# Half-row-block strips with rows of up to 6 KB, 256-column matmuls and row sums spread over three sweeps, in a Chebyshev and SAGE graph kernel

## The reference

```python
h = jnp.maximum(_layernorm(x, axis=-1), 0.0)
terms = [h, adj @ h]
for _ in range(2, 4):
    terms.append(2.0 * (adj @ terms[-1]) - terms[-2])
x = x + jnp.einsum('kni,kio->no', jnp.stack(terms), w_cheb)
h = jnp.maximum(_layernorm(x, axis=-1), 0.0)
deg = jnp.clip(jnp.sum(adj, axis=1, keepdims=True) + 1.0, 1.0, None)
h_neigh = (adj @ h + h) / deg
z = relu(jnp.concatenate([h, h_neigh], axis=1) @ w_sage + b_sage)
x = x + z / jnp.maximum(jnp.linalg.norm(z, axis=1, keepdims=True), 1e-12)
```

## Time and profile before

| | |
|---|---|
| Median of 3 runs | 2655.51 us (2654.42 to 2662.23) |
| Profiled execution | 2672.75 us, its span 2670.9 us |
| PE busy | 2152.7 us (81%) |
| DVE busy | 1637.1 us (61%) |
| ACT busy | 730.2 us (27%) |
| Data read | 686 MB, 258 GB/s over the span |

### The profile page before, as it was taken

One profiled execution on the slowest core, in us unless ns is written; L12 is line 12 of the kernel. 1 busy time (PEld: TensorE's weight loads), 2 busy tenths in 40 slices (PEclk: granted clock), 3 DMA queues, 4 the chain that ended last, 5 costly groups with the idle time before them and its releaser, 6 DMA issues.

```text
span 2670.9 us, 20670 instructions
## 1 busy us (share of the span) xinstructions
PE 2152.7 (81%) x6792; PEld 919.9 (34%) x6792; DVE 1637.1 (61%) x1204; ACT 730.2 (27%) x2243; POOL 821.6 (31%) x1521
## 2 busy tenths in 40 slices
PE   0567778888999999989988979889886897776666
PEld 0123233333334444444434434333332343222222
DVE  2755556656656565756564566766575655576766
ACT  1766666666676674000000000000000000000000
POOL 2222223222322323323222434233232332233423
PEclk9988989999999999999999999889998998888878
DMA  9999999999999999999999999999999999999994
GB/s 206 259 261 265 274 262 268 274 270 268 269 277 276 266 262 258 234 272 238 265 248 259 252 261 257 268 250 269 276 254 268 264 272 267 271 264 270 248 258 127
DMA packets 326445, 689.56 MB, mean 258 GB/s; under 512 B 56514, under 2 KB 93378, under 8 KB 326338
## 3 DMA queue, kind: packets, MB, share of 16 engines
q1 hardware_dynamic: 216832, 344.03, 56.8%
q0 software_dynamic: 108672, 344.03, 46.1%
q10 hardware_dynamic: 834, 0.20, 0.0%
HBM read 685.97 MB, written 2.10 MB: 258 GB/s over the span
## 4 chain that ended last, share of the span: by engine, by line
PE 30%; DMA 29%; SPq 28%; ACT 5%; DVE 5%; issue 2%; POOL 0%; DVEq 0%; ACTq 0%
DMA ring<-in_adj_dram 28%; SPq L317 27%; PE ps_pair L745 23%; ACT ring L393 5%; PE ps_single L751 4%; DVE ring L601 3%; SPq L306 1%; DMA res<-in_x_dram 1%; PE ps_lin L690 0%; PE ps_lin L693 0%; PE ps_lin L706 0%; PE ps_tr L709 0%; PE ps_lin L698 0%; PE ps_xt L642 0%; PE ps_single L652 0%
## 5 line engine op out<-in xcount | busy, mean ns | idle before, releaser
L601 DVE STREAM_TRANSPOSE ring<-ring 128x2048 f32<-128x2048 f32 x640 | 1431.6, 2284 | 810.2 <-DMA ring<-in_adj_dram 536.6
L745 PE MATMUL ps_pair<-ring,vec 128*128 128x512 f32 x2880 | 1319.3, 616 | 151.8 <-DVE ring L601 140.4
L351 POOL DMA_DIRECT2D ring<-in_adj_dram x1448 | 786.0, 551 | 1811.9 <-PE ps_pair L745 1131.1
L745 PEld LDWEIGHTS ps_pair<-ring,vec 128*128 128x128 f32 x2880 | 559.4, 198 | 878.6 <-issue 766.5
L751 PE MATMUL ps_single<-ring,vec 128*64 128x512 f32 x2240 | 591.1, 665 | 285.2 <-DVE ring L601 281.2
L393 ACT ACTIVATE ring<-ring 128x512 f32<-128x512 f32 x1024 | 628.0, 615 | 297.3 <-DMA ring<-in_adj_dram 297.3
L751 PEld LDWEIGHTS ps_single<-ring,vec 128*64 128x64 f32 x2240 | 159.6, 149 | 644.9 <-issue 423.9
L420 ACT ACTIVATE sum_s<-ps_single 128x512 f32<-128x512 f32 x64 | 37.7, 590 | 616.7 <-PE ps_pair L745 449.5
L393 ACT ACTIVATION_READ_ACCUMULATOR ring<-ring 128x1 f32 x1024 | 192.0, 188 | 0.0
L422 ACT ACTIVATE sum_p<-ps_pair 128x512 f32<-128x512 f32 x45 | 26.6, 591 | 452.2 <-PE ps_pair L745 452.2
L431 ACT ACTIVATE stat<-stat 128x4 f32<-128x4 f32 x16 | 3.3, 205 | 258.7 <-DVE stat L554 258.7
(11 more groups left out here) (95 smaller groups left out, 576.7 us busy)
## 6 DMA issues: line engine op xcount, KB each, us to landing
ring<-in_adj_dram POOLq DMA_DIRECT2D x1160, 256.0 KB, 12.1
ring<-in_adj_dram SPq DMA_DIRECT2D x1160, 256.0 KB, 18.4
ring<-in_adj_dram POOLq DMA_DIRECT2D x96, 192.0 KB, 11.2
ring<-in_adj_dram SPq DMA_DIRECT2D x96, 192.0 KB, 18.6
ring<-in_adj_dram POOLq DMA_DIRECT2D x96, 128.0 KB, 10.9
ring<-in_adj_dram SPq DMA_DIRECT2D x96, 128.0 KB, 13.9
ring<-in_adj_dram SPq DMA_DIRECT2D x96, 64.0 KB, 15.2
ring<-in_adj_dram POOLq DMA_DIRECT2D x96, 64.0 KB, 10.2
```

The source lines that it names most:

```text
L351: pool.dma_start(dst, src).then_inc(s_high[i % NSEM], 16)
L601: nc.vector.transpose(blocks, blocks).then_inc(s_turned, 1)
L745: last = nc.tensor.matmul(ps_pair[n % 2][:], vec[:, CB * J + c, :, :], moving, start=(k == pair_at[0] and c == 0), stop=(k == pair_at[-1] ...
```

## The change

A row block is loaded in two halves h (H = 2), each with 8 instead of 16 row groups, in strips up to 12 column blocks wide. The ring keeps its 128 KB and counts 32 half blocks. `split` cuts a row into equal strips of at most 12. A unit is now two neighbouring half blocks (GROUP = 2), again 2048 elements a partition for one transpose; the matmuls write 256 columns, one half of the PSUM tile. The group that needs the newest row, and the diagonal group of sweep 1, go to the end of the row (`behind`). Row sums are taken in sweep 1 only for the half of the columns that doesn't hold the diagonal, the rest in sweeps 2 and 3. SP takes over the stores of the output, POOL has loads alone. x is loaded by SP and ACT, half each, and POOL begins with adj only when x is there. Cut to its core:

```diff
-W = 4
-SW = NB // W
+H = 2
+GH = G // H
+HN = BN // H
-RING = 16
+RING = 32
+WIDE = 12
+GROUP = 2
-STORE_LAG = 6
+STORE_LAG = 12
+SUM_LEAD = 4
@@ class Row
+        for k, (_, J0, w) in enumerate(pieces):
+            groups = [list(range(J, min(J + GROUP, J0 + w))) for J in range(J0, J0 + w, GROUP)]
+            for Js in (reversed(groups) if sweep == 2 else groups):
+                (behind if latest in Js or self.has_late and C in Js else early).append((k, Js))
+        self.units = early + behind
...
+    def summed(self, k):
+        _, J0, w = self.pieces[k]
+        own = NB // 2 * (self.C // (NB // 2))
+        if self.sweep == 1:
+            return None if J0 <= self.C < J0 + w else (J0, J0 + w)
+        if self.sweep == 2:
+            lo, hi = max(J0, self.C + 1), min(J0 + w, own + NB // 2)
+        elif self.sweep == 3:
+            lo, hi = max(J0, own), J0 + w
+        else:
+            return None
+        return (lo, hi) if lo < hi else None
+
+def split(first, last):
+    n = last - first + 1
+    parts = -(-n // WIDE)
+    at = [first + n * k // parts for k in range(parts + 1)]
+    return [(at[k], at[k + 1] - at[k]) for k in range(parts)]
@@ sweep_rows
-        order = [(C // W + 1 + k) % SW for k in range(SW)]
+        runs = [(0, NB // 2), (NB // 2, NB // 2)]
+        if C and C - 1 < NB // 2:
+            runs.reverse()
+        rows.append(Row(1, C, [(h, J0, w) for J0, w in runs for h in range(H)], C - 1))
...
+        runs = split(first, NB - 1)
+        rows.append(Row(2, C, [(h, J0, w) for J0, w in reversed(runs) for h in range(H)], C + 1))
...
+        rows.append(Row(3, C, [(h, J0, w) for J0, w in split(0, C) for h in range(H)], C - 1))
@@ sync
-            for h in range(2):
-                for a in range(Q):
-                    sp.dma_start(res[32 * a:32 * a + 32, 32 * h:32 * h + 32, :], x_v[a, :, 32 * h:32 * h + 32, :])\
-                        .then_inc(s_x[h], 16)
+            for a in range(Q):
+                sp.dma_start(res[32 * a:32 * a + 32, 0:32, :], x_v[a, :, 0:32, :]).then_inc(s_x[0], 16)
...
+                if free_at[i] > 0:
+                    sp.wait_ge(s_unit, free_at[i])
+                at = CB * rows[n].C + CB // H * h
                 for ar in range(Q):
                     for a in (0, 1):
                         col = a * QN + J0 * UC
+                        sp.dma_start(strip_of(i)[32 * a:32 * a + 32, ar:GH:Q, :],
+                                     adj_v[ar, :, at:at + CB // H, col:col + w * UC]).then_inc(s_low[i % NSEM], 16)
@@ gpsimd
+            for h in range(2):
+                pool.wait_ge(s_x[h], 16 * Q)
@@ scalar
+            for a in range(Q):
+                act.dma_start(res[32 * a:32 * a + 32, 32:64, :], x_v[a, :, 32:64, :]).then_inc(s_x[1], 16)
...
+                    for g in range(GH):
+                        cells = strip_of(i)[:, g, (lo - J0) * UC:(hi - J0) * UC]
+                        last = nc.scalar.activation(cells, cells, ACT.Copy,
+                                                    accum_out=into[:, GH * h + g:GH * h + g + 1])
@@ vector
-                    if row.sweep == 1:
-                    dve.wait_ge(s_summed, i + 1)
+                    if i in sum_strips:
+                        dve.wait_ge(s_summed, sum_strips.index(i) + 1)
...
+                    blocks = strip_of(i)[:, :, col:col + len(Js) * UC].rearrange("p g (c q) -> p g c q", q=32)
+                    last = nc.vector.transpose(blocks, blocks)
@@ tensor
+                    cells = slice(HN * h, HN * h + HN)
+                    for J in Js:
+                        for c in range(CB):
...
+                                last = nc.tensor.matmul(ps_pair[n % 2][:, cells], vec[:, CB * J + c, :, :], moving,
+                                                        start=(pair == 0), stop=(pair == pairs - 1))
```

More of the change, by code:

```diff
@@ L92, in sweep_rows @@
     for C in reversed(range(NB)):
-        strips = []
         first = C + 1 if C < LATE_BLOCKS else C
[L95 to L101, removed]
-    for C in range(NB):
[L103 to L131, removed]
+        runs = split(first, NB - 1)
@@ new lines, in sweep_rows, with upper @@
+        rows.append(Row(2, C, [(h, J0, w) for J0, w in reversed(runs) for h in range(H)], C + 1))
+    def upper(C, first, last):
+        return [(h, J0, w) for J0, w in split(first, last) for h in range(H)]
+    half, W = NB // 2, NB // 4
+    for C in range(NB):
+        rows.append(Row(3, C, [(h, J0, w) for J0, w in split(0, C) for h in range(H)], C - 1))
+        if W <= C < 2 * W:
+            D = 2 * W - 1 - C
+            rows.append(Row(4, D, upper(D, D, W - 1), None, final=False))
+        if C >= half:
+            D = NB - 1 - C
+            rows.append(Row(4, D, upper(D, max(D, W), (half if D >= W else NB - W) - 1), None, final=False))
@@ L133, in sweep_rows @@
     for C in [0, 8, 4, 9, 1, 5, 10, 15, 6, 2, 11, 14, 12, 3, 7, 13]:
-        rows.append(Row(4, C, upper(C, max(C, half if C >= W else NB - W), NB - 1)))
+        rows.append(Row(4, C, upper(C, max(C, half if C >= W else NB - W), NB - 1), None))
     return rows
@@ L140, in ring_places @@
     at, places, live = 0, [], []
-    for i, (_, _, w, _) in enumerate(strips):
+    for i, (_, _, _, w) in enumerate(strips):
         if at + w > RING:
@@ L216, in sem @@
             return ctx.enter_context(nc.semaphore(name))
-        ring = sb("ring", [P, RING * G * UC])
+        ring = sb("ring", [P, RING * GH * UC])
         vec = sb("vec", [P, CH, 2, F])
@@ L327, in _ @@
                                     pattern=[[-1, P]], channel_multiplier=1).then_inc(s_const, 1)
-            def store_row(n, C):
-                pool.wait_ge(s_row, n + 1)
-                for a in range(Q):
[L333 to L345, removed]
+            for h in range(2):
+                pool.wait_ge(s_x[h], 16 * Q)
+            for i, (n, h, J0, w) in enumerate(strips):
+                if free_at[i] > 0:
+                    pool.wait_ge(s_unit, free_at[i])
+                at = CB * rows[n].C + CB // H * h
                 for ar in range(Q):
@@ L582, in _ @@
             begun = ended = 0
+            seen = set()
             u = 0
[L584 to L614 removed]
@@ L714, in _ @@
             for n, row in enumerate(rows):
-                pair_at = [k for k, (_, kind) in enumerate(row.units) if kind == PAIR]
-                single_at = [k for k, (_, kind) in enumerate(row.units) if kind == SINGLE]
+                pairs = sum(CB for _, Js in row.units for J in Js if row.kind(J) == PAIR)
+                singles = sum(CB for _, Js in row.units for J in Js if row.kind(J) == SINGLE)
+                pair, single = 0, 0
                 single_slot = {1: 0, 2: 1, 3: 0, 4: 1}[row.sweep]
@@ L719, in _ @@
                     pe.wait_ge(s_x0, 4)
-                strip_of_unit = [i for i in range(first_strip[n], first_strip[n + 1]) for _ in strips[i][3]]
-                for k, (J, kind) in enumerate(row.units):
-                    i = strip_of_unit[k]
-                    J0 = strips[i][1]
+                for k, (piece, Js) in enumerate(row.units):
+                    i = first_strip[n] + piece
+                    _, h, J0, _ = strips[i]
                     if pending < n and u == epilogue_at[pending]:
@@ new lines, in _ @@
+                    cells = slice(HN * h, HN * h + HN)
+                    for J in Js:
+                        for c in range(CB):
+                            chunk = (J - J0) * UC + 32 * c
+                            moving = strip_of(i)[:, :, chunk:chunk + 32]
+                            if row.has_late and J == row.C:
+                                moving = diagonal(J, c)[:, GH // 2 * h:GH // 2 * h + GH // 2, :]
+                            if row.kind(J) == PAIR:
+                                last = nc.tensor.matmul(ps_pair[n % 2][:, cells], vec[:, CB * J + c, :, :], moving,
+                                                        start=(pair == 0), stop=(pair == pairs - 1))
+                                pair += 1
+                            else:
+                                side = F * (c % 2)
+                                last = nc.tensor.matmul(ps_single[n % 2][side:side + F, cells],
+                                                        vec[:, CB * J + c, single_slot, :], moving,
+                                                        start=(single < 2), stop=(single >= singles - 2))
+                                single += 1
```

225 lines of the change are left out of this document (109 added, 116 removed).

## The result

The changed kernel takes 2885.88 us (median of 4 runs, 2884.05 to 2904.49) against 2654.97 before: ratio 1.088, 95% interval 1.083 to 1.093. I had forecast 2275, and the mechanism of none of my rivals gives 2886. The span of the profiled execution is 2885.2 us.

What follows compares the result with a forecast made beforehand. Transfers were taken as the bound, at about 270 GB/s, to rise to 410. Stages of 2131 us plus 158 of late loads gave a 2289 us span, median about 2275; range 2150 to 2440.

Steps and rivals of the forecast that it cites:

- the rate of 410 GB/s: Transfers of strips of 5 blocks or more: both queues move equally, up to 2 x 205 GB/s, 2.56 us a unit.
- the 158 us of late loads: Loads that start only when a row ends, in sweeps 1 to 3: 11 to 27 us in named rows, 30 elsewhere.
- Rival 1: Both queues together stay near 305 GB/s: 2261 us, or 2370 with start, end and late loads; chance 0.28.
- What bounds the kernel now: In the old kernel: transfers at about 270 GB/s, 2554 of 2671 us; two-to-one packet sharing leaves SP alone at 205.
- The stages: Whole kernel: start 47, sweep 1 774, sweep 2 450, sweep 3 570, last units 265, end 25; together 2131 us.
- ACT: the term that was sized wrong: Activations fall from about 630 to 580 us, beside other work; up to 8.3 us in the path at late strips.
- PE, 256 columns: Pair and single units: doubled matmuls and weight loads cost nothing, 0.11 us loads hidden under 0.215 us of streaming.
- rival 3: Pair and single units: shorter matmuls don't hide the weight loads, giving 3070 us; chance 0.05.
- Start: Loading of x: about 20 us without POOL's loads, PE begins at 47 us instead of 77.58.
- Rival 2: Transfers: row size doesn't matter or packets stay two to one, 273 GB/s remain, 2650 us; chance 0.05.
- I am wrong if the slices of sweep 1 stay below 290: Refuting sign for the forecast: the profile's sweep 1 slices staying under 290 GB/s.
- The one for 350 GB/s or more: Confirming sign: 350 GB/s or more in stretches with both queues on 8-block strips, against a ceiling near 310.

Runs made afterwards that it cites:

- e1: Kernel of adj loads only, no computation, with the DMA shapes of both kernels: 209 GB/s for one queue in its own half, 303 for both at 4 KB.
- e9: Changed kernel with ScalarE summing the second strip of each sweep 1 row earlier (look-ahead 5 units instead of 4): 2831.15 us, ratio 1.062.
- e11: Kernel before without the row sums of adj (degrees left out): 2654.78 us beside 2660.45, ratio 0.998.
- e6: Kernel before with each 512-column matmul of a unit as two of 256 columns with the same weights: 2657.67 us beside 2658.23, ratio 0.999.
- e4: Changed kernel with WIDE = 8 instead of 12, nothing else: 2720.16 us, ratio 1.025.
- e12: Changed kernel with WIDE = 4, NSEM = 8, the earlier sum in sweep 1 and row 0 taking columns from its diagonal first: 2561.36 us, ratio 0.962.

## Why the prediction was wrong

Two steps failed: the rate of 410 GB/s, and the 158 us of late loads, in which the sums stand too. The second cost more. Rival 1, which has no 410, still came to only 2370: 2261 us of transfers at 305 GB/s and 110 us besides. Measured were 2444 us in which transfers move (at 282 on the average) and 441 in which they stand still.

**What bounds the kernel now: right in the numbers, wrong in one reading.** Transfers bound it, at two levels near 300 and 205, and the shares go with the packet size, though not quite two to one (e1: 190 and 114 at 2 KB, even at 4 KB). The first step that failed is "Together that would be 410". With even shares, where that reading gives 410, e1 moved 303, and the changed kernel 282 on the average while it moved. The rows couldn't tell 205 and half of it from a common limit near 300, as both give the 308, and no row stood above 321. Rival 1 had this part right in the main; the stretches at 331 and 344 are above its limit, and the average, with narrow strips and one queue alone at times, is below it.

**The stages.** With 0.304 instead of 0.41, sweep 1 needs 883 us of transfers alone (forecast 774 for the stage) and sweep 2 428 beside 450 of PE. The forecast's transfers had slack to pay for standing still (317 beside 450 of PE in sweep 2); at the real rate there is next to none.

**What is late next: the mechanism right, the sum of 158 us far too small.** I named the 11 and 12 block rows of sweep 2 at 21 and 27 us. PE's gap at the first was 29 (above), and the longest, 34.4, stands at 1436 us before the 12-block row. At 274 instead of 410 GB/s the first half strip (5.8 MB) takes 21 us instead of 14, which is the difference. But I counted only PE's wait for the first strip and not the transfers' wait for the row's end, 0 to 6 GB/s at 1370 us. In all the transfers stood still 441 us, 382 more than before. Where they are the bound, that is lost time whatever PE does then. Rival 1 failed by the same step: it gave late loads 65 us and said 2370. WIDE = 8 alone gave 166 us back, WIDE = 4 another 43 without sums.

**ACT: the term that was sized wrong.** I held the sums to be beside other work, up to 8.3 us where a strip is late. They cost 183 us. The total of ACT did fall, as forecast (628.0 to 574.6 us). What counted for 55 of the 183, by e9, is that a sum stands in order behind a wait for PE and ahead of the transpose without which PE can't finish the strip and free its space. The others are open in detail. Before, DVE waited 273 us for the same sums, the transfers went on, and e11 shows that it cost nothing.

**PE, 256 columns: right.** e6 shows the doubling as free, and rival 3 fell; in the changed kernel 64 pair matmuls of 256 columns, each with its weight load, take 13.98 us, 0.218 each. **Start: right**, 42 instead of 47, worth 14 us on the kernel before. **Rival 2** (row size doesn't matter) was near the truth for the sum of both queues and wrong for their shares.

**The signs.** "I am wrong if the slices of sweep 1 stay below 290" was of little use: five of the 15 slices stand at 297 to 306 and ten below 290. And it could not tell the forecast from rival 1, whose 305 passes it too. The one for 350 GB/s or more in stretches with both queues did tell: 299 at 442 us, and 344 at the most over 50 us.

The 231 us are a gain and larger losses. Without sums and with strips up to 4 the same kernel takes 2515, 140 us less than before, and the medians of the table go from there to 2886 in three steps: 43 for strips up to 8 (with two strips fewer in flight), 145 for strips up to 12, 183 for the sums. Measured alone, from the changed kernel, the width is worth 166 (e4) and the place of one sum 55 (e9). Both together were only tried with further edits (e12), where the loss turns into a gain.

## What to carry to other kernels

When a measured rate fits a model of shares, ask what a plain ceiling would give for the same rows, and time the loads alone before building on more than was ever seen. Where transfers are the bound, look in the schedule for the moments at which no load may be issued, and count each as lost, hidden behind compute or not. After the run, split the span into the time in which transfers move and the time in which they don't: the first tells of their rate, the second of the schedule. Before an in-order engine's work is called hidden, read what it waits for just before it.

## What the runs showed of the hardware

- Loads of 32 partitions by one queue into partitions 0 to 63 or 64 to 127 ran at 209 GB/s, two queues each with its own half at 303 to 304, with 2 KB and 4 KB rows alike, by SP and POOL or SP and ACT (299) (e1). In the kernels the same loads also ran at 331 to 344 for 50 us at a time; why isn't known.
- With the halves mixed in each queue, one queue ran at 245 and two at 239 to 249; in the kernels that cost 7.6% and 7.9% (3114.10 against 2885.88, from two sets of runs).
- At 8 KB rows the two queues ran at 278 GB/s, at 512 B rows at 240 (e1). In the kernel strips of 11 blocks (5.5 KB) ran at 274 and strips of 12 (6 KB) at 281 to 294, so the rate doesn't simply fall with the row.
- Splitting 512-column float32 matmuls into 256 columns with a weight load each cost nothing (ratio 0.999).
